# Two stages of a fused transformer block: the order of GpSimd's requests for q, k and v, and unpadded projections with another order of a batch in the second attention

## The reference, cut to what matters

```python
def _fff(x, nw, nb, w1, b1, w2, b2, act):
    node = zeros
    for _ in range(8):
        logit = einsum('bsd,bsd->bs', x, nw[node]) + nb[node]
        node = 2 * node + 1 + (logit > 0)
    leaf = node - 255
    h = act(einsum('bsd,bsdl->bsl', x, w1[leaf]) + b1[leaf])
    return einsum('bsl,bsld->bsd', h, w2[leaf]) + b2[leaf]

def _L1_xattn_ref(x, y, wq, bq, wk, bk, wv, bv, wo, bo):   # 16 heads of 16
    q, k, v = heads(x @ wq + bq), heads(y @ wk + bk), heads(y @ wv + bv)
    attn = softmax(einsum('bhqd,bhkd->bhqk', q, k) / sqrt(16))
    return join(einsum('bhqk,bhkd->bhqd', attn, v)) @ wo + bo
```

## Time and profile before

| what | us |
|---|---|
| median of 3 runs (1478.77 to 1485.66) | 1479.96 |
| the profiled execution | 1475.21 |
| its span, first to last instruction | 1473.2 |
| around the span | 2.0 |
| busy: TensorE / VectorE / ScalarE / GpSimd | 84% / 60% / 40% / 30% |
| mean granted TensorE clock | 0.909 |

### The profile page before, as it was taken

How to read it: one execution, slowest core, us unless ns; L and a number is a source line. 1 busy time by engine, 2 the same in 40 slices (tenths; PEclk the granted TensorE clock), 3 DMA queues, 4 the chain that set the end, 5 groups by cost and what they waited for, 6 DMA issues and landing times. The chain is left out here.

```text
span 1473.2 us, 24697 instructions
## 1 busy us (share of the span) xinstructions
PE 1235.5 (84%) x7236; PEld 899.8 (61%) x7236; DVE 883.5 (60%) x2513; ACT 582.3 (40%) x1106; POOL 446.1 (30%) x588
## 2 busy tenths in 40 slices
PE   1297999999876885897888849589999889999997
PEld 1195777777665764675667737466666555555554
DVE  7998989999613674655454457354556425444534
ACT  2124565665321233464553227144565531212110
POOL 2258344555552045443434327321121000000000
PEclk9658999999988988898989879788999889999999
DMA  9000000000001812758347316710000000000000
GB/s 277 2 2 2 1 1 1 1 1 1 0 1 23 287 55 80 247 176 279 106 124 248 124 40 126 204 15 8 9 9 8 1 1 1 14 0 14 0 15 14
DMA packets 85380, 92.70 MB, mean 63 GB/s; under 512 B 19400, under 2 KB 70090, under 8 KB 85260
## 3 DMA queue, kind: packets, MB, share of 16 engines
q1 hardware_dynamic: 72972, 66.05, 14.2%
q0 software_dynamic: 12288, 25.18, 7.1%
HBM read 76.51 MB, written 14.68 MB: 62 GB/s over the span
## 5 line engine op out<-in xcount | busy, mean ns | idle before, releaser
L3399 ACT ACTIVATE m_silu<-m_psG 128x512 f32<-128x512 f32 x48 | 28.7, 597 | 215.3 <-PE m_psU L3519 215.3
L3452 DVE TENSOR_TENSOR m_act<-m_silu,m_psU 128x512 f32<-128x512 f32 x48 | 33.0, 688 | 122.4 <-ACT m_silu L3399 107.7
L2191 PE MATMUL gq_psH<-gq_xT,gq_w 128*128 (+1 forms) x564 | 100.6, 304 | 4.3 <-ACT gq_w L1898 2.8
L2074 DVE SCALAR_TENSOR_TENSOR gq_hT<-gq_xT,unit_leaf,gq_act 128x128 f32<-128x128 f32 x141 | 49.8, 353 | 84.7 <-ACT gq_act L1906 58.5
L2191 PEld LDWEIGHTS gq_psH<-gq_xT,gq_w 128*128 128x128 f32 x564 | 80.8, 204 | 30.0 <-issue 25.9
L2201 PE MATMUL gq_psY<-leaf_w,gq_hT 128*128 (+1 forms) x282 | 90.9, 406 | 4.8 <-DVE gq_hT L2074 4.6
L3519 PE MATMUL m_psG<-m_xnT,m_gate 128*128 128x512 f32 x192 | 92.0, 602 | 2.1 <-PEq L192 2.1
L3519 PE MATMUL m_psU<-m_xnT,m_up 128*128 128x512 f32 x192 | 90.6, 594 | 0.0
L1792 POOL DMA_INDIRECT gq_x<-rows_x,gq_token_i x48 | 46.0, 958 | 118.4 <-DVE gq_tile_row L2067 62.3
L765 DVE MATCH_REPLACE8 s_product_a_rest<-a_top,s_product_a_rest 128x256 f32<-128x256 f32 x192 | 76.1, 408 | 0.3 <-issue 0.3
L205 POOL TENSOR_SCALAR m_rstd<-m_mean_var 128x4 f32<-128x4 f32 x4 | 0.9, 231 | 240.1 <-DVE m_mean_var L1297 240.1
(11 more groups left out here) (554 smaller groups left out, 3098.2 us busy)
## 6 DMA issues: line engine op xcount, KB each, us to landing
leaf_w<-in_group_w SPq DMA_DIRECT2D x128, 128.0 KB, 3.9
leaf_w<-in_group_w SPq DMA_DIRECT2D x64, 256.0 KB, 4.9
a_w<-in_L_xattn_W SPq DMA_DIRECT2D x2, 1024.0 KB, 12.0
rows_x<-token_rows SPq DMA_DIRECT2D x8, 256.0 KB, 4.8
sorted_y_q<-gq_y SPq DMA_DIRECT2D x16, 128.0 KB, 4.8
sorted_y_k<-rows_ahead SPq DMA_DIRECT2D x16, 128.0 KB, 5.0
sorted_y_v<-gq_y SPq DMA_DIRECT2D x16, 128.0 KB, 2.0
rows_f<-token_rows SPq DMA_DIRECT2D x8, 256.0 KB, 2.7
```

The costliest lines, as they stand in the source:

```text
L2074: dve.scalar_tensor_tensor(hT[n % 2][:], xT[:, DC, bass.ds(g * -P + u * P, P)], leaves.unit_leaf[:, bass.ds(g, 1)], act_h[n % 2][:], ALU.i ...
L2191: last = pe.matmul(psH[n % 2][:, 0:P], w1[n % 3][:, c, :], xT[:, c, bass.ds(g * -P + u * P, P)], start=(c == 0), stop=(c == DC - 1))
```

## The change

It touches two stages.

*q, k, v.* `RING` is 11; the side and leaf buffers of the routing lie in the space of `w1` and `act`, which frees the room. GpSimd's order is another, and a request waits for the one two before it, whichever kind it was. The sorting of q's tokens is moved up in the routing loop.

```diff
-    RING = 6 if nf > 1 else NT
+    RING = 11 if nf > 1 else NT
...
-        self.side = [sb(f"side{n}", [P, 2, S], BF16) for n in range(2)]
-        self.leaf = [sb(f"leaf{n}", [P, 2, S], BF16) for n in range(2)]
+        self.side, self.leaf = spaces[0:2], spaces[2:4]
...
-                    if n >= 2:
-                        pool.wait_ge(tile_in[(n - 2) % RING], 16 * ((n - 2) // RING + 1))
+                    if len(under_way) >= 2:
+                        pool.wait_ge(*under_way[-2])
+                    under_way.append((tile_in[n % RING], 16 * (n // RING + 1)))
...
-                    for t in range(RING):
+                    for t in range(NT):
                         gather(0, t)
-                    for t in range(NT):
                         seed(0, t)
-                    for t in range(RING, NT):
-                        gather(0, t)
                     for f in range(1, nf):
+                        for t in range(RING):
+                            gather(f, t)
                         for t in range(NT):
                             seed(f, t)
-                        for t in range(NT):
+                        for t in range(RING, NT):
                             gather(f, t)
```

```diff
-    LOADS = 7 + H1
+    LOADS = 7 + 16 + H1
-        load(wq[:], dram["c_wq"].rearrange("(c p) n -> p c n", p=P))
-        load(wk[:], dram["c_wk"].rearrange("(c p) n -> p c n", p=CP))
+        for w, name, rows in ((wq, "c_wq", P), (wk, "c_wk", CP)):
+            for c in range(2):
+                load(w[:, c, :].rearrange("p (h d) -> p h d", d=DH1),
+                     dram[name][c * rows:(c + 1) * rows].rearrange("p (h k) -> p h k", k=32)
+                     [:, :, 0:DH1])
-        load(bq[:], dram["c_bq"])
-        load(bk[:], dram["c_bk"])
+            for h in range(H1 // 2):
+                at, column = 32 * (h % 4), h // 4
+                for bias, name in ((bq, "c_bq"), (bk, "c_bk")):
+                    load(bias[h * DH1:(h + 1) * DH1, :],
+                         dram[name][at:at + DH1, column::2])
...
                 def head_product(out, w, src, n, signal):
-                    for c in range(2):
-                        at = (2 * n + c) * P
-                        for k in range(2):
-                            last = pe.matmul(out[:, c, :], w[:, k, at:at + P], src(k),
-                                             start=(k == 0), stop=(k == 1))
+                    for k in range(2):
+                        last = pe.matmul(out[:, n, :], w[:, k, n * P:(n + 1) * P], src(k),
+                                         start=(k == 0), stop=(k == 1))
...
+                    for c in (2 * n, 2 * n + 1):
+                        last = dve.tensor_scalar(kT[b % QK_SLOTS][:, c, :], KEYS[:, n, :],
+                                                 own_rows[:, c % 2:c % 2 + 1], bk[:, c:c + 1],
+                                                 ALU.mult, ALU.add)
...
-                for j in range(4):
-                    pool.wait_ge(ready, 1 + j)
-                    pool.affine_select(out=bk[:], in_=bk[:], compare_op=ALU.not_equal, fill=-1.0,
+                pool.wait_ge(spread, SPREAD)
+                for j in range(8):
+                    pool.wait_ge(ready, 1 + j)
+                    pool.affine_select(out=bk[:, j % 2::2], in_=bk[:, j % 2::2],
```

More of the change, by code:

```diff
@@ L1457, with __init__ @@
     ITEMS = B + 2 * B
-    def __init__(self, core, ctx, tokens, leaves, places, rows, nw, xnT, banks):
+    def __init__(self, core, ctx, tokens, leaves, places, rows, nw, xnT, banks, spaces):
         self.core, self.tokens, self.leaves = core, tokens, leaves
@@ L1719, in group_products @@
         w1 = [sb(f"w1_{n}", [P, DC, P]) for n in range(3)]
-        act_h = [sb(f"act{n}", [P, P]) for n in range(2)]
+        acts = sb("act", [P, 2, P])
+        act_h = [acts[:, n] for n in range(2)]
         hT = [sb(f"hT{n}", [P, P]) for n in range(2)]
@@ L1737, in group_products @@
             route = Routing(core, own, tokens, leaves, places, rows, nw, xnT,
-                            (psX, psH, psY[1:3]))
+                            (psX, psH, psY[1:3]),
+                            [part[:].bitcast(BF16) for part in (*w1, acts)])
         pair_base = weights.loads
@@ L2925, in shift_rows @@
                     rows = qT[b % QK_SLOTS][:, 2 * n:2 * n + 2, :]
-                    dve.tensor_tensor(rows, psY[SHIFTS_AT[n]][:], rows, ALU.add
+                    dve.tensor_tensor(rows, (turns(b) if n else KEYS)[:], rows, ALU.add
                                       ).then_inc(m_sb.s, 1)
@@ L2976, in _ @@
                         maximum(b, 1)
+                        values(b)
+                        shift_rows(b, 0)
                     if 0 <= p < B:
@@ L3001, in x_turned @@
                     reached(pe, norm, b)
-                    if b:
-                        reached(pe, v_sb, b - 1)
+                    if b > 2:
+                        reached(pe, at_sb, b - 3)
+                    elif b == 2:
+                        reached(pe, m_sb, 0, 2)
+                    out = beside(b - 1) if b else turns(0)
                     for t in range(ST):
                         for c in range(DC):
-                            last = pe.transpose(psY[1][:, c, t * P:(t + 1) * P],
+                            last = pe.transpose(out[:, c, t * P:(t + 1) * P],
@@ L3025, in head_product, with value_product @@
-                def head_product(out, w, src, n, signal):
-                    for c in range(2):
-                        at = (2 * n + c) * P
-                        for k in range(2):
-                            last = pe.matmul(out[:, c, :], w[:, k, at:at + P], src(k),
-                                             start=(k == 0), stop=(k == 1))
+                def value_product(b, g):
+                    if b > 1 and g == 0:
+                        reached(pe, t_sb, b - 2, 2)
+                    elif b and g == 0:
+                        reached(pe, v_sb, 0)
+                    for k in range(2):
+                        at = b * S + g * P
+                        last = pe.matmul(VALUES[:, g, :], core.ctxT[:, k, at:at + P],
+                                         wv[:, k, :], start=(k == 0), stop=(k == 1))
+                    if g == ST - 1:
+                        last.then_inc(v_ps.s, 1)
```

321 lines of the change are left out of this document (160 added, 161 removed).

## The result

The kernel before took 1479.37 us (median of 4 runs, 1473.67 to 1485.66), the changed one 1444.23 (1436.27 to 1447.87): ratio 0.9737, interval 0.9700 to 0.9775, so 35 us less where I had forecast 59. The range that I gave was 1400 to 1442: 1444.2 lies 2 us above it, and 0.9737 of the 1479.96 that I had started from is 1441.0, just inside. The profiled execution has a span of 1446.1, against 1473.2. It took 1447.87 us and was the slowest of the four, so the two traces are 27 us apart and not 35.

The account below looks back on a forecast made before the run. It took GpSimd's requests to bound q, k, v and TensorE the second attention. Gains 33.3 + 22.4 + 5 - 2 = 58.7 took 1475.21 to 1416.5; the median's 4.75 made 1421, stated as 1420, range 1400 to 1442.

Parts of the forecast that it names:

- q: q, k, v stage: tile and bias requests alternate, first at 520.6, unit 12 at 572.6; gain 10.8 us.
- k and v: q, k, v stage: eleven buffers let tile requests go early; gain 3.1 us in k, 19.4 from k into v.
- rival 1: q, k, v stage: GpSimd's queue keeps v's requests late, half of part 1 goes; 1437 us, chance 0.12.
- A batch: Second attention: a batch takes 23.9 us instead of 27.09; gain 3.2, for seven batches 22.4.
- Start and tail: Second attention's start: earlier projections and a filled wait before a low-clock stretch; gain 5 us, bounds 0 and 10.
- Rival 2: Second attention, first and last batches: two or three low-clock stretches of 6 to 8 us; 1434 to 1442, chance 0.11.
- Rival 3: Second attention, steady batches: waits pull TensorE's clock down; 1496 for half the products, 1576 for all; chance 0.03.
- Loads: SyncE's queue: second attention's loads in 64-byte runs delay the result stores; cost 2 us, 0 to 8.
- Rival 4: SyncE's loads: small runs at 2 to 3 times the price hold stores and start; 1431 to 1445, chance 0.04.
- part 1: q, k, v stage: new request order, eleven buffers and earlier routing steps; gain 33.3 us, bounds 18 and 40.

Follow-up runs that it names:

- three under way: The changed kernel with three GpSimd requests under way instead of two in q, k, v: 1404.7 us, ratio 0.9513.
- Doubling: The changed kernel with each q and k projection product of the second attention done twice over: 1455.2 us, ratio 0.9864.
- halving: The kernel before with only the first half of the contraction of each q and k projection in the second attention: 1473.4 us, ratio 0.9987.
- the first part alone: The kernel before with only eleven tiles, the new request order in q, k, v and the earlier routing steps: 1472.1 us, ratio 0.9956.

## Why the prediction was right and wrong

**q: right at the start, then thinner.** First request forecast 520.6, measured 520.50; unit 12 forecast 572.6, measured 575.24. The requests came at 1.65 us each (520.50 to 571.54), not at 1.54. Of the 8.1 us gained by unit 12, 4.8 were left at the last unit of q (628.51; 633.35 before).

**k and v: the step that failed** is "so all eleven are out by unit 12 of k. The biases of v follow", with its gain of 19.4. That eleven buffers allow the requests is true, but in GpSimd's own queue k's sixteen biases (595.47 to 634.95) and k's five late tiles stand ahead of them. v's eleven went out from 645.47 to 668.48, its biases from 673.18, near the end of k (unit 12 of k was at 649.61). Tile 11 was asked for at 709.98, 23 us into v, where I had 6.5. From unit 43 of k to unit 12 of v it took 41.59 us, so the gain was 2.4. In k, units 0 to 12 took 19.48: 0.5 instead of 3.1. The stage gave 4.9 in the trace, against a bound from below of 18: this is rival 1 ("v's requests stay late"), for which I had taken half of the part away; nearly all of it went. And I had no term for the handover: "The rows fetched ahead for the next stage stand behind the last tile as before" was right, but the next stage waits for them, so nothing of the 4.9 reached it in this trace.

The deeper fault is that I took 1.54 and 2.5 us a request from the earlier trace rows as prices and didn't ask what ended GpSimd's idle time between those rows. It was mostly the landing of the request two back (65.3 us in that kernel, beside 25.9 for TensorE's turning); the few rows that I had picked all happen to show "issue" or another engine. 96 requests at a fixed pace can't end earlier by being put in another order. By the price of issuing alone, 0.95 busy and 0.30 between, three under way then showed what was there to be had. The Trainium skill, "DMA: Bandwidth & Descriptors", Anatomy of one DMA, gives some 2.0 us as fixed cost of a GpSimd transfer, mostly completion, plus bytes at 436 GB/s; for a tile of 131 KB that makes an estimate of 2.3. By it two under way would suffice for one request each 1.25 us. The measurements differ: the profile of the kernel before has tiles landing 2.7 to 5.6 us after the issue, 2.9 in the median, and in the changed kernel the third request of q went out at 523.78, after a wait of 0.76 us for the first, 3.3 us after it. Two for each 3.3 us are the 1.65 us a request of q.

**A batch: right.** 23.9 forecast, 24.27 measured; the score buffer's chain is next, and the gain is less than the full 3.64 for the reason given: handovers at 0.2 to 0.3 us. From keyed product to scores I had 3.23 and 2.6 or 2.9 behind; the rows show 3.24 (1062.81 to 1066.05) and 2.58 (1060.23 to 1062.81). Scores that read 32 rows take 1.15 us like those that read 16, as I had costed them. Doubling and halving showed that neither edit alone does it.

**Start and tail: right in kind, too small.** I took 5 us, with 10 as a bound. From the last sum of f to the first exponential it went from 43.71 to 38.88, the first batch from 34.26 to 26.41, six further batches from 163.43 to 144.51, and from there to the first silu from 33.65 to 29.45: 35.8 in all, against 22.4 + 5. The tail wasn't in my sum. There the clock was 0.86 in the stretch from 1140 to 1190 before and 1.00 after.

**Rival 2, low clock in the head,** came in part: from 940 to 990 the clock was 0.62 on average (0.75 in the kernel before, where the earlier trace rows had shown 0.50 near the end of it), and the head was shorter all the same.

**Rival 3, the clock in steady batches,** did not come: 1.00 throughout, with four waits a batch behind products that cycle through banks. What the Trainium skill ("TensorE: Matmul & The Clock Gate", A second HAM failure mode) tells of another kernel does not happen on this trace at waits of 0.2 to 0.3 us, nor in the halved kernel at 0.6 to 1.0.

**Loads: cheaper.** SyncE's issues in the changed kernel:

```profile
894.85 1.92 SPq L2671 DMA_DIRECT2D c_wq<-in_c_wq  x2
896.81 3.01 SPq L2671 DMA_DIRECT2D c_wk<-in_c_wk  x2
...
913.32 7.48 SPq L2671 DMA_DIRECT2D c_wo<-in_c_wo  x16
...
924.91 14.35 SPq L1847 DMA_DIRECT2D sorted_y_f<-gf_y  x16
```

The 7,168 runs of 64 bytes held its queue 4.9 us, where leaf_b's runs of 8 bytes had made me take 10.5. The queue was free at 920.8; the stores ended at 939.26, 0.8 us after f's last sum: they waited for sums, and the loads cost the stores nothing. Rival 4 is out.

The sum, then: 33.3 for part 1 was 4.9 at v's last sum and nothing at the start of the next stage in this trace, 8 in the run of the first part alone; 27.4 for the second attention was 35.8, and the 2 for the loads did not come. The errors are of opposite sign, 25 us or more on the one side and 8 on the other, and network f's 7.5 us in this trace are in no term. That the measured time came out at the edge of the range is luck: the mechanism of part 1, more than half of the sum, was wrong, and a gain in the tail for which I had no term made up for some of it.

## What to carry to other kernels

When a chain of requests sets the pace, read what ends the idle time before each of them before reordering it. Here it was the landing of an earlier one: order and buffers moved the stall, and what moved the end was the number under way and, by a few us, an earlier start. Try that number one step at a time, since here three gave 33 to 40 us and four cost 57. Follow the chain to its very end, too: the next stage may wait for its last request and not for the last sum. Where an engine is full and a shared buffer is nearly so, taking work away and reordering are worth little apart and 2.8 us of 27 together.

## What had not been expected of the hardware

Three indirect requests of GpSimd under way, 1.29 us apart in q, disturbed nobody; four, 1.25 us apart, stopped VectorE and ScalarE for 10 to 16 us at a time, and the kernel took 1501.7 us instead of 1404.7. In twelve of the fourteen traces the token attention began 12.1 us after GpSimd's last request of the stage before. And loads in runs of 64 bytes cost SyncE 0.69 ns each (4.93 us for 7,168), less than half of the 1.47 of 8-byte runs (12.04 us for 8,192).
